# Second attention: softmax weights turned by transposing DMAs as pairs of 16-bit numbers, instead of by TensorE

## The reference, cut to what matters

```python
x = x + _L1_attn_ref(_layernorm(x, axis=-1), Wq, Wk, Wv, Wo)
# in it: H, Dh = 16, 128, T = 2048
q, k, v = ((x @ W.T).reshape(B, T, H, Dh) for W in (Wq, Wk, Wv))
q, k = _apply_rope(q, cos, sin), _apply_rope(k, cos, sin)
scores = einsum('bthd,bshd->bhts', q, k) * Dh ** -0.5
attn = softmax(where(causal, scores, -inf), axis=-1)
y = einsum('bhts,bshd->bthd', attn, v).reshape(B, T, H * Dh)
return y / 3.0 @ Wo.T
```

## Time and profile before

| | |
|---|---|
| median of 3 runs | 2009.21 us (2007.48 to 2012.58) |
| span of the profiled execution | 2012.9 us (its own time is not given apart from the span) |
| instructions | 40239 |
| TensorE busy | 1931.8 us, 96% |
| DVE busy | 1433.8 us, 71% |
| ACT busy | 1315.8 us, 65% |
| POOL busy | 939.7 us, 47% |
| granted TensorE clock, mean | 0.997 |

### The profile page before, as it was taken

The page is one execution under the profiler, slowest core; times in us unless marked ns, Lnnn a source line. Parts: engine busy times, 40 slices in busy tenths (PEclk is TensorE's granted clock), DMA queues, the critical chain, the costliest instruction groups (busy, mean ns, idle before and its releaser), DMA issues.

```text
span 2012.9 us, 40239 instructions
## 1 busy us (share of the span) xinstructions
PE 1931.8 (96%) x13726; PEld 1757.7 (87%) x13726; DVE 1433.8 (71%) x3587; ACT 1315.8 (65%) x3367; POOL 939.7 (47%) x961
## 2 busy tenths in 40 slices
PE   6888989998999999999999999999999999999899
PEld 5678857787999999999999999999999999998888
DVE  8378653756878778687877868787777878777753
ACT  4346533444778677777867777787777778776652
POOL 2641126534554636545463554545365554536242
PEclk9999999999999999999999999999999999999999
DMA  8750177500000000000000000000000000000000
GB/s 292 195 100 2 48 241 172 121 1 9 9 9 6 10 7 4 7 9 9 7 9 7 4 7 9 9 7 9 7 4 7 9 9 7 9 6 2 22 27 32
DMA packets 58600, 73.44 MB, mean 36 GB/s; under 512 B 9760, under 2 KB 45216, under 8 KB 58272
## 3 DMA queue, kind: packets, MB, share of 16 engines
q1 hardware_dynamic: 48032, 58.03, 9.0%
q0 software_dynamic: 10368, 12.85, 3.9%
HBM read 51.06 MB, written 19.80 MB: 35 GB/s over the span
## 4 chain that ended last, share of the span: by engine, by line
PE 60%; DVE 11%; ACT 9%; POOL 7%; issue 7%; DMA 0%; ACTq 0%; another core or an unknown queue 0%; POOLq 0%; DVEq 0%
PE phase_scores L1271 16%; PE phase_ring L1329 9%; PE phase_y L167 5%; PE phase_y L166 5%; PE phase_y L165 5%; PE phase_ring L165 4%; PE phase_ring L167 4%; PE phase_ring L166 4%; ACT phase_p L1303 4%; DVE phase_scores L1282 2%; POOL phase_rot L2511 2%; POOL phase_straight L2509 2%; PE phase_up_ps L165 2%; PE phase_up_ps L167 1%; PE phase_up_ps L166 1%
## 5 line engine op out<-in xcount | busy, mean ns | idle before, releaser
L1303 ACT ACTIVATE phase_p<-phase_scores,phase_bias 128x512 f32<-128x512 f32 (+3 forms) x680 | 417.5, 628 | 117.4 <-DVE phase_bias L1291 116.8
L1349 DVE TENSOR_TENSOR phase_pt_lo<-phase_ring,phase_pt_hi 128x512 fp32r<-128x512 f32 (+3 forms) x680 | 390.7, 603 | 90.4 <-ACT phase_pt_hi L1344 86.5
L1344 ACT ACTIVATE phase_pt_hi<-phase_ring 128x512 fp32r<-128x512 f32 (+3 forms) x680 | 343.1, 536 | 105.1 <-PE phase_ring L1329 101.7
L1329 PE MATMUL phase_ring<-sb_ident,phase_p 128*128 128x128 f32 x2312 | 340.5, 273 | 13.0 <-ACT phase_p L1303 7.4
L165 PE MATMUL phase_y<-phase_pt_hi,phase_v_hi 128*128 128x256 f32 (+1 forms) x1152 | 341.2, 296 | 6.7 <-DVE phase_y_lo L2485 6.7
L167 PE MATMUL phase_y<-phase_pt_hi,phase_v_lo 128*128 128x256 f32 (+1 forms) x1152 | 321.2, 279 | 0.0
L166 PE MATMUL phase_y<-phase_pt_lo,phase_v_hi 128*128 128x256 f32 (+1 forms) x1152 | 321.2, 279 | 0.0
L1329 PEld LDWEIGHTS phase_ring<-sb_ident,phase_p 128*128 128x128 f32 x2312 | 271.6, 140 | 54.3 <-ACT phase_p L1303 17.7
L1284 DVE TENSOR_REDUCE phase_peaks<-phase_scores 128x1 f32<-128x512 f32 (+1 forms) x408 | 265.8, 666 | 46.0 <-PE phase_scores L1271 43.6
L2509 POOL TENSOR_TENSOR phase_straight<-phase_rot,late_rope 64x512 f32<-64x512 f32 x128 | 164.0, 1281 | 275.2 <-ACT phase_rot L2378 275.1
L2526 POOL TENSOR_TENSOR sb_x<-sb_x,phase_part 128x512 f32<-128x512 f32 x128 | 165.1, 1290 | 252.8 <-ACT phase_part L2413 246.4
(11 more groups left out here) (292 smaller groups left out, 4836.3 us busy)
## 6 DMA issues: line engine op xcount, KB each, us to landing
y_rows<-phase_zero SPq DMA_DIRECT2D x16, 512.0 KB, 7.6
phase_e_up<-expert_up SPq DMA_DIRECT2D x16, 352.0 KB
phase_e_dn<-expert_down SPq DMA_DIRECT2D x16, 256.0 KB
xn_rows<-phase_ln_xn SPq DMA_DIRECT2D x8, 512.0 KB, 2.9
sb_x<-y_rows POOLq DMA_DIRECT2D x8, 512.0 KB, 6.6
late_raw_qk<-qk SPq DMA_DIRECT2D x16, 256.0 KB, 2.7
phase_logits_t<-expert_up SPq DMA_DIRECT2D x8, 352.0 KB
phase_ln_xn<-expert_up SPq DMA_DIRECT2D x8, 352.0 KB
```

The lines of the kernel that those rows point to most:

```text
L1303: act.activation(self.p[:, at:at + width], self.scores[:, at:at + width], ACT.Exp, bias=self.bias[:, t % 2:t % 2 + 1], accum_out=self.sums ...
L1329: done = pe.transpose(bank[:, j * P:(j + 1) * P], self.p[:, (4 * place + j) * P:(4 * place + j + 1) * P], self.core.ident[:])
L1344: act.activation(hi, value, ACT.Copy).then_inc(*self.t_hi.one)
L1349: dve.tensor_tensor(lo, value, as_f32(hi), ALU.subtract).then_inc(*self.t_lo.one)
```

## The change

The turn step changes hands. TensorE and the ring take no part in it any more, and `turn` is replaced in `RING` by `bound`, which happens once in two heads.

- ACT copies the chunk of `p` from SBUF, times 2^14, into a 16-bit float (`act_split`); DVE writes p · 2^14 less that as a second 16-bit float with one scalar_tensor_tensor (`dve_split`). Both lie in one of eight rooms of `split`. The exp now waits for DVE's remainder of the chunk four before, where it waited for TensorE's transpose.
- SP issues one transposing DMA per chunk, from `split` into `pt`, which has three rooms for pairs of tiles (`sp_turn`). It waits for DVE's remainder and for the pv that read the room last. These DMAs stand in SP's list in the place of the turn, among the weight loads.
- pv takes its moving operands from `pt` and waits for each chunk's DMA (`pe_wait_laid`). v is also kept as two 16-bit floats, scaled by a power computed from the weights: a sum of squares of the value weights (ACT), a small matmul (`bound`), DVE and a power on POOL; `share` puts the inverse scale into the output weights. This runs once in two heads.
- Some semaphores are shared between stages to keep their number down, and the loads of the next stage's first weights are issued from within the list of turns. At the end ACT waits for all laid rooms before it takes over the next stage's weights.

```diff
-    RING = ("project", "values", "turn", "out", "flip", "next_flip")
+    RING = ("project", "values", "bound", "out", "flip", "next_flip")
+    SPLIT_ROOMS, PAIR_ROOMS, SHARE = 8, 3, 2.0 ** 14
+    def turned_rooms(self, sb):
+        self.split = sb("split", [P, self.SPLIT_ROOMS, 4, 2, P], F16)
+        self.turned_rest = sb.rest()
+        self.pt = sb("pt", [P, self.PAIR_ROOMS, NT, 2, 2 * P], F16)
...
-        self.v_hi, self.v_lo = (sb(n, [P, NT, 2 * DH], F32R) for n in ("v_hi", "v_lo"))
+        self.v_hi, self.v_lo = (sb(n, [P, NT, 2 * DH], F16) for n in ("v_hi", "v_lo"))
...
+    def p_read(self, key):
+        return self.t_lo[key]
...
+    def act_split(self, act, key):
+        hi, lo, value = self.split_views(key)
+        act.wait_ge(*self.p_done[key])
+        if (n := self.turn_at[key]) >= self.SPLIT_ROOMS:
+            act.wait_ge(*self.laid[n % self.SPLIT_ROOMS][self.turns[n - self.SPLIT_ROOMS]])
+        act.activation(hi, value, ACT.Copy, scale=self.SHARE).then_inc(*self.t_hi.one)
+    def dve_split(self, dve, key):
+        hi, lo, value = self.split_views(key)
+        dve.wait_ge(*self.t_hi[key])
+        dve.scalar_tensor_tensor(lo, value, self.SHARE, hi, ALU.mult, ALU.subtract).then_inc(*self.t_lo.one)
+    def sp_turn(self, sp, key):
+        h, t, b = key
+        keys, r = self.blocks(t, b), self.turn_at[key] % self.SPLIT_ROOMS
+        sp.wait_ge(*self.t_lo[key])
+        if old := self.old_pair(*key):
+            sp.wait_ge(*old)
+        out = self.pt[:, self.pair_room(h, t // 2), keys.start:keys.stop, :, (t % 2) * P:(t % 2 + 1) * P]
+        sp.dma_start_transpose(out.rearrange("p j s q -> p (j s) q"),
+                               self.split[:, r, 0:len(keys)].rearrange("p j s k -> p (j s k)")).then_inc(*self.laid[r].one)
+    def pe_wait_laid(self, pe, h, g, j):
+        for t in (2 * g, 2 * g + 1):
+            if j <= t and (j == 0 or self.chunk(t, j) != self.chunk(t, j - 1)):
+                key = h, t, self.chunk(t, j)
+                pe.wait_ge(*self.laid[self.turn_at[key] % self.SPLIT_ROOMS][key])
...
-                if j % 4 == 0:
-                    pe.wait_ge(*self.t_lo[h, 2 * g + 1, j // 4])
+                self.pe_wait_laid(pe, h, g, j)
...
-                         [(self.pt_hi[buf][:, j, q], self.pt_lo[buf][:, j, q])], first=j == 0, last=j == 2 * g + 1).then_inc(*self.weighed.one)
+                         [(self.pt[:, room, j, 0, q], self.pt[:, room, j, 1, q])], first=j == 0, last=j == 2 * g + 1).then_inc(*self.weighed.one)
...
+        if name == "wv":
+            if n >= 2:
+                act.wait_ge(*self.bounded[n - 2,])
+            act.activation(self.core.squares[:], raw[:].rearrange("p k h -> p (k h)"), ACT.Square,
+                           accum_out=self.core.power[:, n % 2:n % 2 + 1]).then_inc(*self.squared.one)
...
             elif what == "turn":
-                self.dve_turn(dve, key)
+                self.dve_split(dve, key)
```

More of the change, by code:

```diff
@@ L2154, in __init__ @@
             s.plan(ends)
+        turns = of("turn")
+        self.turns, self.turn_at = turns, {key: n for n, key in enumerate(turns)}
+        self.laid = [core.loads(f"filled{r}") for r in range(self.SPLIT_ROOMS)]
+        for n, key in enumerate(turns):
+            self.laid[n % self.SPLIT_ROOMS].plan([key])
+        self.filled = core.flag("attn_ones")
+        self.filled.plan([tag])
+        self.squared, self.bounded, self.bound_kept = sig("wv_squared"), sig("wv_bound"), sig("wv_kept")
+        self.v_scaled, self.spread_done, self.shared = sig("v_scale"), sig("spread"), sig("wo_scale")
+        self.squared.plan(of("bound")[1:])
+        for s in (self.bounded, self.bound_kept, self.v_scaled):
+            s.plan(of("bound"))
+        for s in (self.spread_done, self.shared):
+            s.plan(of("share"))
         self.follower = None
@@ L2203, in plan_order @@
                     elif letter == "w" and h % 2:
-                        steps = [("load_wv", h // 2 + 1)]
+                        steps = [("load_wv", h // 2 + 1), ("bound", h // 2 + 1)]
+                    elif letter == "u" and h % 2:
+                        steps = [("share", h // 2 + 1)]
                     elif letter == "l":
@@ L2210, in plan_order @@
                         steps = [next(late)]
-                    order += [step for step in steps if 0 <= step[1] < (NH // 2 if step[0] in ("values", "load_wv") else NH)]
+                    order += [step for step in steps if 0 <= step[1] < (NH // 2 if step[0] in ("values", "load_wv", "bound", "share") else NH)]
         order.append(("out", NH - 1, G - 2))
@@ L2223, in ring_read @@
             return norm.lo[(norm.tag, *step[1:])]
-        return {"turn": self.t_lo, "project": self.rotated, "values": self.v_lo_done, "out": self.parted}[step[0]][step[1:]]
[L2226 to L2230, removed]
-        return self.weighed[h, g, min(keys[-1], 2 * g + 1)] if h >= 0 else None
+        return {"bound": self.bound_kept, "project": self.rotated, "values": self.v_lo_done, "out": self.parted}[step[0]][step[1:]]
@@ L2312, in pe @@
                 self.pe_score(pe, key, pairs)
-            elif what == "turn":
-                self.pe_turn(pe, key)
+            elif what == "bound":
+                n, = key
+                pe.wait_ge(*(self.squared[key] if n else self.prior.next_squared[self.tag]))
+                if n == 0:
+                    pe.wait_ge(*self.filled[self.tag])
+                self.pe_ring_wait(pe, step)
+                pe.matmul(self.ring_bank(step)[:, 0:1], self.ones[:], core.power[:, n % 2:n % 2 + 1], start=True, stop=True).then_inc(*self.bounded.one)
             elif what == "values":
@@ L2492, in pool @@
             what, key = step[0], step[1:]
-            if what == "stats":
+            if what == "bound":
+                n, = key
+                pool.wait_ge(*idle)
+                pool.wait_ge(*self.bound_kept[key])
+                if n >= 2:
+                    pool.wait_ge(*self.v_lo_done[n - 2, G - 1])
+                    pool.wait_ge(*self.shared[n - 2,])
+                pool.tensor_tensor(self.v_scale[:, n % 2:n % 2 + 1], self.bound[:, n % 2:n % 2 + 1], self.core.half[:, 0:1], ALU.pow).then_inc(*self.v_scaled.one)
+                idle = self.v_scaled[key]
+            elif what == "stats":
                 pool.wait_ge(*idle)
```

102 lines of the change are left out of this document (77 added, 25 removed).

## The result

The changed kernel takes 2363.36 us (median of 4, 2359.26 to 2366.49) against 2009.3 us: a ratio of 1.1758, interval 1.1739 to 1.1777. It is 354 us slower. The direction was forecast, but the forecast was 2040, 31 us slower; its own range, 2015 to 2180, missed the time, and only the wide range of 1915 to 2430 held it.

The account below looks back on a forecast made before the run. TensorE was taken as the bound, 87.9 of 88.55 us a head; afterwards 84.8 + 5 = 89.8 a head, +20 over sixteen, and 8 at the ends gave 2037, say 2040; own range 2015 to 2180, 8-in-10 range 1915 to 2430.

Parts of the forecast that it names:

- the terms per engine: Second attention, work a head after the change: TensorE 70 us, ACT 68, DVE 80.3.
- The lock: DVE remainders with two SBUF inputs wait while POOL works: 12.9 us a head, DVE 67.4 to 80.3.
- The signs named in advance: Expected in the profile: remainders' mean well above 603 ns, POOL pieces above 1.29 us, issue to landing near 4 us.
- under 85%: Sign: TensorE busy under 85% in the stage, its longest waits at the pv line for a DMA.
- 0.6 to 0.75: Sign: the share of the DMA engines expected in the second attention.
- SP's queue: Weight loads behind waiting turns cost nothing unless turns fall behind as a whole; the start and end add 8 us together.
- How unevenly the work lies: Largest engine of each PLAN string, summed: 84.8 us a head with waits for POOL, 77.0 without; 88.4 for the kernel before.
- What TensorE loses: Second attention's transposes, 17.9 us a head, leave TensorE; 70 us of its work a head remains.
- What the transposing DMA costs: A full turn is laid 4.1 us behind its remainder; TensorE's waits at pv taken as 5 us a head.
- Rival (c): DMA engines or SP become the bound: 2690 us, or 2190 halfway; chance 0.20 for anything over 2180.
- Rival (a): Faster, the DMA hidden if a full turn lands in under about 3 us: 84.5 us a head, 1950; chance 0.30.
- Rival (b): DVE's waits for POOL do not bite as well: 77 to 79 us a head, 1840; chance 0.06.

Follow-up runs that it names:

- third kernel: The changed kernel with SP's weight loads moved ahead of earlier turns and the bound's small matmul moved later: 2162.02 us, ratio 1.0701.
- without lock and wait: Changed kernel, loads ahead, bound later, two ring banks, remainder's second tensor from PSUM, pv not waiting for the DMA: 1993.09 us, ratio 0.9921.
- the kernel with PSUM: Changed kernel, loads ahead, bound later, two ring banks, remainder's second tensor from a zero-filled PSUM bank, subtraction left out: 2009.58 us, ratio 0.9964.

## Why the prediction was right in direction and wrong in size

**Right: the terms per engine.** DVE was forecast at 80.3 us a head and works 80.9, 81.2 and 80.6 (after, third kernel, and kernel before with two SBUF tensors). The lock's 0.32 us for a remainder, added to 603 ns, gives 925 ns; 930 is measured. The Trainium skill's rule of "SBUF — State Buffer", Who interferes with whom, weighed against the earlier trace rows in the prediction, held: 154 us go when the second tensor leaves SBUF. The signs named in advance came too, remainders well above 603 ns and longer pieces of POOL. TensorE was 74% busy in the eight heads, as "under 85%" said, though not by the wait that was named. The DMA's share there was 0.47, under the 0.6 to 0.75 that was named.

**Failed: "SP's queue".** The step said that the loads behind the turns "have a fraction of a head to spare, so they cost nothing unless the turns fall behind as a whole". They cost 198 of the 354 us. The spare time was counted on a queue that ran far ahead of the engines, as the earlier trace rows and the idle SP of before allow. Once SP waits for each remainder (959.8 us in all), it is at the engines' own place in the list, and whatever stands there is issued only when it is wanted: turns of 1.23 us each ahead of it, 0.57 to issue, 2.8 to land for q and k. The step looked for a loss of throughput; the loss was of lead. All engines run dry, and in the windows shown TensorE comes back at the lower clock. How much of the 198 us is the clock's is open: no run held it apart. For the same 11566 matmuls TensorE is busy 1852.1 us in the changed kernel and 1797.6 with the loads ahead.

**Failed: "How unevenly the work lies".** The count by strings gave 84.8 with the lock and 77.0 without. Measured with the loads mended and the DMA's microsecond taken off: 96.3 and 86.9, 11.5 and 9.9 more. A part of that is a term of "What TensorE loses": 70 us a head, where TensorE is busy 79.6 in the third kernel (clock 0.91) and 75.3 without lock and wait (0.97). Put into the same count, these add about 3 and 2 us, an estimate. The other 8 to 9 are in no engine's work. The argument that the count "can be trusted", since it gave 88.4 where 88.55 was measured, was no test: before, TensorE is 99% busy in those heads, and any count holds then. My account of the rest, argued and only in part tested, is a ring of waits. The change took TensorE's work away and left the ring: exp frees a bank, scores fill it, DVE takes the maximum behind the remainders that stand ahead in its list, the bias follows, and the next exp. Its length isn't any engine's sum. Longer remainders would lengthen it at once, which fits the 123 us in a kernel that TensorE bounds by its work; and less work for TensorE would hardly shorten it, which fits 2010 with both causes removed. What is shown is that order alone, with the same work, moves the time from 2089 to 2462. But a fifth bank gave only 1%, where the ring was expected to give 2 to 6%, and the same reasoning had promised a gain from the turns behind exp. Which link is longest in each string wasn't taken apart.

**Too high: "What the transposing DMA costs".** Forecast 5 us a head, measured 1 with the lock and 0.3 to 0.6 without. The turn lands 3.1 us behind its issue, against 4.1 behind its remainder in the forecast, and longer heads leave it time. When the scores were put first, the DMA's wait rose from 23.0 us to 61.5, and with all turns behind exp to 213.2: it was hidden. The issue, bounded from below by 0.33 us, is 1.23 us of SP, 49 us a head; the sum had it only as 0.33 us of a turn's delay, and it adds to the loads' delay. In the 5 us windows shown above, the engines moved 158 GB/s at the most, at a share of 0.86, so an estimate for full engines is 184. The 261 GB/s of the Trainium skill's "DMA: Bandwidth & Descriptors", Latency and other measured facts, weren't reached in any of them.

**The rivals.** Rival (c), over 2180, had the time but not the cause: the DMA's share is 0.47 and SP issues for 49 us of 111. That the wide range held 2363 is therefore luck: it reached so far only for the sake of (c). Rival (a) had the DMA's cost almost right, and its condition, a landing under about 3 us, was missed by 0.1. Rival (b) is refuted by the remainders of 930 ns. The case that came, a queue that loses its lead, was no rival at all; it was named in a half sentence and priced at nothing.

## What to carry to other kernels

When steps that wait for the engines move onto a queue that used to run ahead, every prefetch behind them loses its lead: put the prefetches ahead of the waiting steps by at least their issue, landing and all that is queued before them. A count by the busiest engine tells the time only while that engine is nearly always busy; once its work is cut, look for the waits between engines that remain (here probably exp, bank, score, maximum, bias) and ask what the change lengthens on them. And two SBUF tensors on DVE beside a busy POOL cost whole waits (930 ns a remainder), where one of them in PSUM costs none (600 ns).

## What the runs showed of the hardware

- A transposing DMA takes SP 1.17 us at least and 1.23 in the median to issue, where the load of the output weights took 0.33 in the kernel before; in the kernel with turns that load takes 0.57:

```profile
L2305 SPq DMA_TRANSPOSE phase_pt<-phase_split x640: 1168/1232/2528, 491.4 to 2255.4; - x160
...
DMA to landing us min/median/max: 2.3/3.1/5.1
```

- A weight load of 128x128 in 16 bits takes 102 ns even at a clock of 0.90, against 189 for the f32 form of the same product in the kernel before:

```profile
L166 PEld LDWEIGHTS phase_y<-phase_pt,phase_v_hi 128*128 128x128 f16 x1152 | 117.9, 102 | 221.7 <-issue 200.0
```

- A scalar_tensor_tensor of 512 elements with one tensor in PSUM and one in SBUF has a mean of 679 ns beside the same POOL work, where two in SBUF have 998 (in the windows of the kernel with PSUM and of the changed one). The first is no more than the 684 that one with two SBUF tensors took in the earlier trace rows, so the lock spares the form with PSUM.
